# Dealing the maxima pieces anew among a quad's half units, and moving its five value batches

## Chip, cores and metric

The kernel runs on one core of a Trainium2 chip. The metric is the device time of one execution in microseconds (us). In the core TensorE (PE) does matrix products, VectorE (DVE) and ScalarE (ACT) read its results out of PSUM, GpSimd (POOL) moves and gathers, SyncE (SP) issues most DMA transfers, and 16 DMA engines carry them.

## What is computed

A layer norm of x (4 x 1024 x 256) feeds an attention of 16 heads of width 16 and a mixture of 8 experts, two of them chosen for each token; the output is x + attention * silu(experts). Cut to the attention, which the change is about:

```python
S = jnp.einsum('hid,hjd->hij', K, Q) * SCALE          # rows are keys' positions
delta = idx[:, None] - idx[None, :]
S = jnp.where(delta < 0, -jnp.inf, S) + decay         # decay is -delta, causal
C = jax.nn.softmax(S, axis=-1)
attn = jnp.einsum('hij,hjd->hid', C, V)
return attn @ o_w.T + o_b
```

## The kernel before

**Stages.** Layer norm and projections run first (to about 127 us of the profiled span), then the attention in 16 quads of four heads (127 to 601 us), then the experts tile by tile and the output. A quad's work stands in `window(q, ...)`, and a "window" below is the stretch from the first half unit of one quad to the first of the next. q runs from 0 to 15.

**Three kinds of work in a window.** The scores are computed twice. First come the *pieces*: score blocks (L1338, with the diagonal mask added by a small product at L1341) from which DVE takes the row maxima (L988). They are computed one quad ahead. A piece lies in one of three PSUM banks and a new one may be written when DVE has reduced the piece three places earlier (`piece_used`). When piece 37, the last of a quad, is reduced, DVE splits the maxima into three bf16 parts (L993 to L1002); the *maxima* item (L1347) turns them, DVE copies them out (L1008), and SP writes them into the key rows of the next quad (L493), which the next window awaits (`m_in`). Second come 36 *half units* (L1387, mask at L1390): the same scores transposed, less the maxima, which ACT exponentiates (L879); they have three banks of their own. Third come five *batches* (`send_batch`, L1401) of value products, one for each of five types of units; batch k waits for the exponentials of its type. ACT copies a quad's finished output out (L863, `evacuate`) after exponential 5 of the next window.

**Order on TensorE.** It is written out by hand in `window`: half unit i, then one item (two at i = 6, 14 and 30, named in `EXTRA_ITEM`), then the batch whose step is i. `BATCH_STEP` puts batch 0 after half unit 10, batch 1 after 18, batch 2 after 26, batch 3 after 34, and batch 4 after half unit 2 of the next window. The 39 items of window q, numbered j0 to j38 here, are always in the same order: j0 to j23 are pieces 14 to 37 of quad q+1; j24 to j27 pieces 0 to 3 of quad q+2; j28 the maxima of quad q+1; j29 to j38 pieces 4 to 13 of quad q+2. By kind: j1 and j24 hold four masked blocks of 128 columns; j6, j7, j25 and j26 two of 256; j12 to j15, j27 and j29 to j31 one of 384; j20 to j23 and j32 to j35 a masked block of 512; the other 15 pieces an unmasked one. In window 0 one item more, the expert counts, stands at place 20.

**Loads.** The operands of quad q+2 are brought in window q by twelve DMAs of 128 KB (`load_rows`, L484), paced on SP by finished half units; after the sixth stands `store_quad` (L500, L501), eight stores of quad q-1 that wait for `evacuate`. Item j24, the first piece of quad q+2, is the first to read them, and waits for all twelve:

```python
if piece == 0:
    pe.wait_ge(aug_in[(n + d) % AUG], 192 * ((q + d) // AUG) + 192)
```

**Waits of ACT on batches.** Exponential 4 of a window writes where batch 4 of the quad before still reads, so it waits for that batch; the exponentials of types 2, 3 and 4 wait in the same way for batches 0, 1 and 2 of their own quad. POOL's `next_v` waits for batch 4 of the quad before as well.

Of the kernel before, what the change touches and what calls it, by code (L numbers as in the profile page):

```python
# [17 lines left out]
TB = T // P  # L18
# [44 lines left out]
BATCH_STEP = (10, 18, 26, 34, NU + 2)  # L63
EXTRA_ITEM = (6, 14, 30)
# [4 lines left out]
assert len(BATCH_STEP) == NTY  # L69
# [8 lines left out]
INVERT_ITEM = 4  # L78

# [12 lines left out]
assert WIN % PIECE_BANKS == 0 and NU % SCORE_BANKS == 0 and WIN == NU + len(EXTRA_ITEM)  # L92
# [97 lines left out]
def attention_moe_kernel(nc, x, wqT, wkT, wvT, woT, qb, kb, vb, ob, gate, w1, b1, w2, b2, alpha,  # L190
# [5 lines left out]
    with ctx:  # L196
        def sb(name, shape, dt=fp32):
            return ctx.enter_context(nc.sbuf_tensor(name, shape, dt))
# [35 lines left out]
        mask_sb = sb("mask_sb", [P, P], bf16)  # L234
# [9 lines left out]
        zeros = sb("zeros", [P, W])  # L244
# [167 lines left out]
        def many_zeros(n):  # L412
            return bass.AP(zeros[:, :].tensor, zeros[:, :].offset,
                           [list(zeros[:, :].ap[0]), [0, n], [1, D]])
# [7 lines left out]
        def _(sp):  # L422
# [5 lines left out]
            def load_x_chunk(b, c):  # L428
# [8 lines left out]
                     "idb": (idb[:, :], ident_b), "mask": (mask_sb[:, :], mask_neg),  # L437
# [199 lines left out]
        def _(pool):  # L637
            pool.sem_inc(split_done, 8)
            nc.gpsimd.memset(zeros[:, 0:D], 0.0).then_inc(zeros_set, 1)
# [18 lines left out]
            pool.dma_start(xs_t[:, SLOTS - ZERO_TILES:SLOTS, 0:D], many_zeros(ZERO_TILES)).then_inc(xs_zero, 16)  # L658
            pool.dma_start(xs_t[:, SLOTS - ZERO_TILES:SLOTS, D:W], spare[:, :, 0:1].bitcast(fp32),
# [65 lines left out]
            def clear_pads(e, q):  # L725

                pool.wait_ge(pads_ready, 1)
                pool.wait_ge(xs_zero, 32 + 16 * e)
                nc.gpsimd.tensor_copy(zeros[:, D:W].bitcast(i32), spare[:, e, 1:2]).then_inc(zeros_set, 1)
                pool.wait_ge(zeros_set, 4 + e)  # L730
                pool.wait_ge(exp_done, NU * q + PADS_STEP + SCORE_BANKS + 1)
                nc.gpsimd.indirect_dma_start(
                    out=xs_dram, in_=zeros[:, :], in_offset=None,
                    out_offset=bass.IndirectOffsetOnAxis(ap=pad_slot[:, e:e + 1], axis=0)).then_inc(xs_zero, 16)
# [16 lines left out]
            for q in range(MOVE_FROM, FIRST_TAIL):  # L751
                r = q - MOVE_FROM
                first_tile, count = MOVES[r], MOVES[r + 1] - MOVES[r]
                pool.dma_start(x_move[:, 0:count, 0:D], xn_t[:, first_tile:first_tile + count, :]).then_inc(x_moved, 16)
                next_v(q, q % AUG)
                pool.wait_ge(x_moved, 16 * r + 16)
                for k in range(2):
                    pool.wait_ge(scattered, 16 * (2 * first_tile + k * count))
                    nc.gpsimd.tensor_copy(x_move[:, 0:count, D:W].bitcast(i32),
                                          y_row[:, first_tile:first_tile + count, k:k + 1]).then_inc(rows_ready, 1)  # L760
# [11 lines left out]
            pool.dma_start(y_row_of[:, :].bitcast(fp32), xs_t[:, 0:SLOTS, D:W].rearrange("p n o -> p (n o)"),  # L772
# [160 lines left out]
        def _(dve):  # L933
# [49 lines left out]
            def reduce_piece(s, banks, piece):  # L983
                dve.wait_ge(piece_done, s + 1)
                ib, lo, h, heads, width = PIECES[piece]
                src = banks[:, 0:heads * width].rearrange("p (h j) -> p h j", h=heads)
                col_ = ib if lo + width == P * (ib + 1) else TB // 2 + ib
                nc.vector.tensor_reduce(mxa[:, h:h + heads, col_], src, AX.X, ALU.max).then_inc(piece_used, 1)  # L988

            def split_maxima(q, s):  # L990

                dve.wait_ge(piece_used, s + PIECE_BANKS + 1)
                nc.vector.tensor_tensor(mxa[:, :, TB // 2:TB], mxa[:, :, TB // 2:TB], mxa[:, :, TB:],  # L993
                                        ALU.max).then_inc(m_step, 1)
# [51 lines left out]
            ahead_of_windows = iter(list(enumerate(stream(0))))  # L1046

# [12 lines left out]
            dve.wait_ge(consts_in, 16 * NCONST)  # L1060
# [219 lines left out]
        def _(pe):  # L1280
# [50 lines left out]
            def send_piece(n, s, banks, piece):  # L1331
# [3 lines left out]
                for h in range(heads):  # L1335
                    out_ = banks[:, h * width:(h + 1) * width]
                    diagonal = lo + width == P * (ib + 1)
                    ins = nc.tensor.matmul(out_, k_aug[n][0:SCORE_ROWS, h0 + h, ib * P:(ib + 1) * P],  # L1338
                                           q_aug[n][0:SCORE_ROWS, h0 + h, lo:lo + width], start=True, stop=not diagonal)
                    if diagonal:  # L1340
                        ins = nc.tensor.matmul(out_[:, width - P:], idb[:, :], mask_sb[:, :], start=False, stop=True)  # L1341
# [111 lines left out]
            for g, step in enumerate(BATCH_STEP):  # L1453
                if step >= NU:
                    send_batch(NQ - 1, (NQ - 1) % AUG, g)
# [134 lines left out]
```

## Time and profile before

| | us |
|---|---|
| median of 3 runs | 805.32 (805.02 to 805.58) |
| the profiled execution | 801.64 |
| its span, first to last instruction | 799.7 |
| windows 3 to 12, each | 29.71 (window 7: 29.88) |
| windows 0, 1, 2 | 32.82, 30.78, 30.47 |
| windows 13, 14, 15 | 32.40, 27.06, 23.84 |

How to read the profile: the page gives the busy share of each engine over the whole span, and the chain of work that ended last. The windows view gives busy time by stretch, the waits view who waited for whom, the timeline the instructions in order. On PE a matmul is pipelined, so its price is the distance from its start to the next start, not its duration. "PEld" is the load of weights, which runs beside the matmuls. A DMA issued by SP shows as "SPq"; its time to landing is from the issue to the semaphore.

### The profile page before, as it was taken

The page shows a single profiled execution, that of the slowest core. Times are in us where ns is not written, and L with a number is a line of the kernel's source. Part 1 is how long each engine was busy: PE and PEld are TensorE (multiplying, and loading weights), DVE is VectorE, ACT ScalarE, POOL GpSimd, SP SyncE. Part 2 cuts the span into 40 slices and gives each one's busy share as a digit, 9 for nine tenths or more (in the row PEclk, how much of TensorE's full clock was granted, in tenths as well). Part 3 has the DMA queues.
Part 4 walks back from the last instruction along what each step waited for, and adds up shares of the span by engine and source line. Part 5 has one row for each costly group of instructions (what it writes and reads, how often), then busy time and mean ns, then how long its engine had stood idle before and what let it go on. Part 6 is the DMA issues. An engine that isn't in the chain of part 4 may idle for free.

```text
span 799.7 us, 16759 instructions
## 1 busy us (share of the span) xinstructions
PE 746.0 (93%) x5575; PEld 447.8 (56%) x5579; DVE 534.0 (67%) x1084; ACT 520.5 (65%) x1044; POOL 245.4 (31%) x311
## 2 busy tenths in 40 slices
PE   4999998999999999999999999989988999999884
PEld 2555553444554554544544544544437899999763
DVE  2456878788777787787787787787404544444287
ACT  3775556576676676676676676666786566666354
POOL 0442232251123223223223222202134457444300
PEclk9999999999999999999999999999999999999998
DMA  8889935254466476486486476495555765555487
GB/s 206 242 204 270 248 127 126 35 107 96 99 121 122 114 143 131 101 146 134 96 146 141 95 139 138 97 141 115 122 93 163 184 187 170 160 168 164 147 289 248
DMA packets 85253, 119.49 MB, mean 149 GB/s; under 512 B 14175, under 2 KB 58719, under 8 KB 85119
## 3 DMA queue, kind: packets, MB, share of 16 engines
q1 hardware_dynamic: 76654, 94.50, 53.0%
q0 software_dynamic: 8528, 24.07, 9.9%
q8 instruction: 41, 0.67, 0.4%
q14 instruction: 30, 0.25, 0.1%
HBM read 72.61 MB, written 45.52 MB: 148 GB/s over the span
## 4 chain that ended last, share of the span: by engine, by line
PE 66%; DVE 12%; DMA 9%; issue 5%; ACT 3%; SPq 2%; POOL 2%; ACTq 0%; POOLq 0%; DVEq 0%
PE ps L1401 15%; PE ps L1338 13%; PE ps L1387 12%; PE ps L1481 8%; PE ps L1503 7%; DVE mxa L988 7%; DMA arena<-y_dram 3%; PE ps L1390 3%; PE ps L1299 2%; PE ps L1341 2%; PE ps L1464 2%; DMA q_parts<-arena 2%; POOL arena L648 2%; DMA aug<-q_parts 2%; ACT arena L879 1%
## 5 line engine op out<-in xcount | busy, mean ns | idle before, releaser
L988 DVE TENSOR_REDUCE mxa<-ps 128x1 f32<-128x512 f32 (+3 forms) x608 | 363.0, 654 | 93.6 <-PE ps L1341 63.4
L879 ACT ACTIVATE arena<-ps 128x512 f32<-128x512 f32 x576 | 312.1, 604 | 148.5 <-PE ps L1390 130.0
L1338 PE MATMUL ps<-aug 105*128 105x512 bf16 (+3 forms) x768 | 228.8, 327 | 12.8 <-DVE mxa L988 9.5
L1387 PE MATMUL ps<-aug 108*128 108x512 bf16 (+3 forms) x768 | 216.2, 327 | 2.3 <-ACT arena L879 0.8
L1401 PE MATMUL ps<-arena,v_q 128*32 128x512 f32 (+3 forms) x1536 | 140.4, 491 | 3.7 <-ACT arena L879 3.7
L1338 PEld LDWEIGHTS ps<-aug 105*128 105x128 bf16 x768 | 74.8, 98 | 81.9 <-DVE mxa L988 34.6
L1387 PEld LDWEIGHTS ps<-aug 108*128 108x128 bf16 x768 | 66.1, 98 | 84.1 <-issue 32.5
L1390 PE MATMUL ps<-maskT_sb,idb 128*128 128x128 bf16 x512 | 112.4, 220 | 0.0
L1341 PE MATMUL ps<-mask_sb,idb 128*128 128x128 bf16 x512 | 98.6, 219 | 0.0
L764 POOL DMA_INDIRECT xs_dram<-arena,slot x64 | 62.8, 982 | 104.8 <-ACT arena L879 91.0
L785 POOL DMA_INDIRECT y_dram<-arena,y_row_of x71 | 68.8, 969 | 73.2 <-DVE arena L1238 72.1
L1401 PEld LDWEIGHTS ps<-arena,v_q 128*32 128x32 f32 x1536 | 41.1, 109 | 68.4 <-issue 49.6
L1481 PE MATMUL ps<-arena 128*128 128x128 f32 x568 | 75.4, 276 | 2.3 <-ACT arena L894 2.3
L1503 PE MATMUL ps<-w_sb,arena 128*128 x284 | 74.1, 384 | 0.5 <-DVE arena L1238 0.5
L1481 PEld LDWEIGHTS ps<-arena 128*128 128x128 f32 x568 | 69.1, 192 | 3.2 <-ACT arena L894 3.1
L1202 DVE TENSOR_TENSOR arena<-ps,arena 128x256 f32<-128x256 f32 x71 | 30.1, 424 | 48.9 <-PE ps L1481 47.5
L906 ACT ACTIVATE arena<-w_sb 128x512 f32 x71 | 44.7, 629 | 24.6 <-issue 23.8
L1390 PEld LDWEIGHTS ps<-maskT_sb,idb 128*128 128x128 bf16 x512 | 49.9, 97 | 18.1
L648 POOL TENSOR_TENSOR arena<-arena 128x512 bf16<-128x512 f32 x32 | 37.0, 1156 | 67.6 <-ACT arena L817 67.6
L1341 PEld LDWEIGHTS ps<-mask_sb,idb 128*128 128x128 bf16 x512 | 50.2, 98 | 6.4 <-issue 3.3
L1238 DVE TENSOR_TENSOR arena<-ps,arena 128x256 f32<-128x256 f32 x71 | 30.1, 424 | 33.1 <-PE ps L1503 28.6
L1503 PEld LDWEIGHTS ps<-w_sb,arena 128*128 128x128 f32 x284 | 48.6, 190 | 5.4 <-issue 1.3
(136 smaller groups left out, 670.6 us busy)
## 6 DMA issues: line engine op xcount, KB each, us to landing
aug<-k_parts SPq DMA_DIRECT2D x96, 128.0 KB, 4.7
aug<-q_parts SPq DMA_DIRECT2D x96, 128.0 KB, 5.2
arena<-xs_dram SPq DMA_DIRECT2D x71, 128.0 KB, 2.7
arena<-y_dram SPq DMA_DIRECT2D x16, 512.0 KB, 4.9
k_parts<-arena SPq DMA_DIRECT2D x16, 384.0 KB, 5.9
q_parts<-arena SPq DMA_DIRECT2D x16, 384.0 KB, 4.4
arena<-in_x SPq DMA_DIRECT2D x8, 512.0 KB, 6.2
xn_dram<-arena SPq DMA_DIRECT2D x8, 512.0 KB, 8.1
```

Source lines behind the costliest of these rows:

```text
L648: nc.gpsimd.tensor_tensor(parts[c][n][:, 2, :], whole[c][n], parts[c][n][:, 1, :], ALU.subtract).then_inc(split_done, 1)
L764: nc.gpsimd.indirect_dma_start(out=xs_dram, in_=x_move[:, s, :], in_offset=None, out_offset=bass.IndirectOffsetOnAxis(ap=slot[:, first_til ...
L785: nc.gpsimd.indirect_dma_start(out=y_dram, in_=ysb[n % STEP], in_offset=None, out_offset=bass.IndirectOffsetOnAxis(ap=y_row_of[:, n:n + 1] ...
L879: nc.scalar.activation(probs[SLOT[k, u]][:, half], score_bank(q, i), ACT.Exp).then_inc(exp_done, 1)
L988: nc.vector.tensor_reduce(mxa[:, h:h + heads, col_], src, AX.X, ALU.max).then_inc(piece_used, 1)
L1338: ins = nc.tensor.matmul(out_, k_aug[n][0:SCORE_ROWS, h0 + h, ib * P:(ib + 1) * P], q_aug[n][0:SCORE_ROWS, h0 + h, lo:lo + width], start=T ...
L1341: ins = nc.tensor.matmul(out_[:, width - P:], idb[:, :], mask_sb[:, :], start=False, stop=True)
L1387: ins = nc.tensor.matmul(out_, q_aug[n][0:ALL_ROWS, h, jb * P:(jb + 1) * P], k_aug[n][0:ALL_ROWS, h, i0:i0 + hi - lo], start=True, stop=lo ...
L1390: ins = nc.tensor.matmul(out_[:, 0:P], idb[:, :], maskT_sb[:, :], start=False, stop=True)
L1401: ins = nc.tensor.matmul(ps[2 * HD * h:2 * HD * (h + 1), 6 * BANK + lo:6 * BANK + hi], v_q[n][:, jb, h, :], probs[SLOT[k, u]][:, at_:at_ + ...
L1481: ins = nc.tensor.matmul(bank(2 + j % 2)[:, m * P:(m + 1) * P], w1_now[j % 2][:, k, m * P:(m + 1) * P], xgT[j % CH][:, k * P:(k + 1) * P], ...
L1503: ins = nc.tensor.matmul(bank(6 + j % 2)[:, 0:D], hid[j % CH][:, k * P:(k + 1) * P], w2_sb[:, e * KT + k, :], start=(k == 0), stop=(k == K ...
```

## The change

Only TensorE's order is changed in substance. The table `ITEMS_AFTER` says how many items follow each half unit (0 to 3), `BATCH_AFTER` after which half unit a batch is sent, and `ITEMS_BEFORE_BATCH` how many of that step's items go ahead of it. Batch 4 of the quad before moves from half unit 2 to 4, batch 0 stays at 10, batch 1 moves from 18 to 22, batch 2 stays at 26, batch 3 moves from 34 to 33. The order of the items among themselves and that of the half units are the same, and so are the programs of DVE and ACT. Written out (h half unit, j item, B batch), the window becomes:

```
h0 h1 j0 j1 h2 h3 j2 j3 h4 j4 [B4 of the quad before] j5 h5 j6 j7 h6 h7 j8 j9 h8 j10 h9 j11 h10 [B0]
j12 j13 h11 j14 h12 j15 h13 h14 j16 j17 h15 j18 h16 h17 j19 h18 j20 h19 j21 h20 h21 j22 h22 j23 j24 [B1]
j25 h23 j26 h24 j27 j28 h25 h26 j29 [B2] h27 h28 j30 h29 j31 j32 h30 j33 h31 h32 j34 j35 h33 j36 [B3]
h34 j37 h35 j38
```

Beside it, small things: the mask and a block of zeros share one tile (`blank`), so the mask begins at another address; a row of `xs_dram` holds its index in column 0 and its data in columns 1 to 256, where the index was last; DVE's wait for the constants stands ahead of its second batch of projections, where it stood behind the last; `masked_by_vector` always returns False, so the path it opens on DVE is not taken; `MERGED` is 4, so the merge of maxima has the columns it had.

```diff
-BATCH_STEP = (10, 18, 26, 34, NU + 2)
-EXTRA_ITEM = (6, 14, 30)
+ITEMS_AFTER = (0, 2, 0, 2, 2, 2, 0, 2, 1, 1, 2, 1, 1, 0, 2, 1, 0, 1, 1, 1, 0, 1, 3, 1, 2, 0, 1, 0, 1, 2, 1, 0, 2, 1, 1, 1)
+BATCH_AFTER = (4, 10, 22, 26, 33)
+ITEMS_BEFORE_BATCH = (1, 0, 2, 1, 1)
...
+def masked_by_vector(piece):
+
+    ib, lo, h, heads, width = PIECES[piece]
+    return False
...
-        mask_sb = sb("mask_sb", [P, P], bf16)
...
-        zeros = sb("zeros", [P, W])
+        blank = sb("blank", [P, W + P // 2])
+        zeros = blank[:, 1:W]
+        wide_mask = blank[:, :].bitcast(bf16)
+        mask_sb = wide_mask[:, 2 * W:2 * W + P]
...
-                sp.dma_start(xg[j], xs_dram[bass.ts(n, P), 0:D]).then_inc(xg_in[j], 16)
+                sp.dma_start(xg[j], xs_dram[bass.ts(n, P), 1:W]).then_inc(xg_in[j], 16)
...
+            dve.wait_ge(zeros_set, 1)
+            dve.wait_ge(consts_in, 16 * NCONST)
...
             def window(q, n, base, items, first=False):
                 sent = 0
-                pe.wait_ge(m_in, 48 * q + 48)
-                for i in range(NU):
-                    half_unit(q, n, i)
-                    for _ in range(2 if i in EXTRA_ITEM or first and i == COUNTS_STEP else 1):
+
+                def send_items(count):
+                    nonlocal sent
+                    for _ in range(count):
                         held = q == NQ - 2 and i < MAXIMA_STEP and sent < len(items) and items[sent][0] == "maxima"
                         if sent < len(items) and not held:
                             send(q, n, base + sent, piece_bank(base, sent), items[sent])
                             sent += 1
-                    if i in BATCH_STEP:
-                        send_batch(q, n, BATCH_STEP.index(i))
-                    elif NU + i in BATCH_STEP and not first:
-                        send_batch(q - 1, (n - 1) % AUG, BATCH_STEP.index(NU + i))
-
+
+                pe.wait_ge(m_in, 48 * q + 48)
+                for i in range(NU):
+                    half_unit(q, n, i)
+                    count = ITEMS_AFTER[i] + (first and i == COUNTS_STEP)
+                    if i not in BATCH_AFTER:
+                        send_items(count)
+                        continue
+                    b = BATCH_AFTER.index(i)
+                    send_items(ITEMS_BEFORE_BATCH[b])
+                    if b > 0:
+                        send_batch(q, n, b - 1)
+                    elif not first:
+                        send_batch(q - 1, (n - 1) % AUG, NTY - 1)
+                    send_items(count - ITEMS_BEFORE_BATCH[b])
```

## Rows read from the trace of the kernel before

**Rows 1.** The page's busy time and share of each engine.
```profile
PE 746.0 (93%) x5575; PEld 447.8 (56%) x5579; DVE 534.0 (67%) x1084; ACT 520.5 (65%) x1044; POOL 245.4 (31%) x311
```

**Rows 2.** Windows view, windows 6 and 13: busy us (count) by engine, granted clock, DMA share.
```profile
309.88:339.59 29.71, 29.39 (x259) 14.67 (x258) 23.52 (x44) 20.36 (x38) 8.84 (x12) 1.00 0.66 126
518.03:550.43 32.40, 29.65 (x258) 14.64 (x256) 26.16 (x48) 21.17 (x38) 2.84 (x2) 1.00 0.99 160
```

**Rows 3.** PE's timeline in window 6: start, duration, line, shape.
```profile
312.87 0.38 PE L1338 MATMUL ps<-aug 105*128 105x512 bf16 x1
313.09 0.38 PE L1387 MATMUL ps<-aug 108*128 108x512 bf16 x1
313.30 0.22 PE L1390 MATMUL ps<-maskT_sb,idb 128*128 128x128 bf16 x1
313.36 0.38 PE L1338 MATMUL ps<-aug 105*128 105x512 bf16 x1
...
317.34 1.92 PE L1401 MATMUL ps<-arena,v_q 128*32 128x512 f32 x16
319.20 0.39 PE L1387 MATMUL ps<-aug 108*128 108x384 bf16 x2
```

**Rows 4.** The same timeline about j24, the piece before the maxima item, and the next window.
```profile
327.53 0.23 PE L1338 MATMUL ps<-aug 105*128 105x128 bf16 x1
...
329.98 0.34 PE L1338 MATMUL ps<-aug 105*128 105x384 bf16 x1 [0.30 <-DVE mxa L988]
...
339.59 0.38 PE L1387 MATMUL ps<-aug 108*128 108x512 bf16 x1
```

**Rows 5.** DVE's timeline in window 6: reductions and the split of the maxima.
```profile
313.29 5.47 DVE L988 TENSOR_REDUCE mxa<-ps 128x1 f32<-128x512 f32 x9 [0.73 <-PE ps L1338]
...
328.14 0.17 DVE L993 TENSOR_TENSOR mxa<-mxa 128x16 f32<-128x16 f32 x1
...
329.23 2.35 DVE L988 TENSOR_REDUCE mxa<-ps 128x4 f32<-128x512 f32 x4
```

**Rows 6.** ACT's timeline in window 6: the evacuation.
```profile
314.59 1.03 ACT L863 ACTIVATE arena<-ps 128x1024 f32<-128x1024 f32 x1
```

**Rows 7.** SP's issues in window 6: load 7, load 12.
```profile
318.59 0.33 SPq L484 DMA_DIRECT2D aug<-k_parts  x1
...
321.90 0.32 SPq L484 DMA_DIRECT2D aug<-q_parts  x1
```

**Rows 8.** Tile view of the twelve loads, windows 3 and then 6: us to landing.
```profile
DMA to landing us min/median/max: 3.2/3.8/5.0
...
DMA to landing us min/median/max: 4.1/4.9/5.6
```

**Rows 9.** The chain that ended last: start, us, what; the last load of windows 7 and 12.
```profile
351.61 6.16 DMA aug<-q_parts
...
500.34 6.19 DMA aug<-q_parts
```

**Rows 10.** Waits for these loads in windows 0, 7 and 13: us in total, times, longest.
```profile
PEld ps L1338 <- DMA aug<-q_parts: 0.4, 1, 0.4
...
PEld ps L1338 <- DMA aug<-q_parts: 0.9, 1, 0.9
...
PEld ps L1338 <- DMA aug<-q_parts: 1.6, 1, 1.6
```

**Rows 11.** PE's timeline: j24 in window 13.
```profile
538.60 0.23 PE L1338 MATMUL ps<-aug 105*128 105x128 bf16 x1 [1.27 <-DMA aug<-q_parts]
```

**Rows 12.** Windows view, window 6 from 2 to 15 us after its start.
```profile
311.88:324.88 13.00, 13.00 (x103) 5.81 (x99) 11.12 (x20) 9.48 (x18) 4.50 (x7) 1.00 1.02 165
```

**Rows 13.** ACT's timeline in window 15, which has no items: its idle time before each stretch.
```profile
584.82 4.03 ACT L879 ACTIVATE arena<-ps 128x512 f32<-128x512 f32 x8 [1.02 <-PE ps L1390]
```

**Rows 14.** PE's longest idle time late in the kernel, and the granted clock behind it.
```profile
761.25 0.59 PE L1516 MATMUL ps<-arena,before_sb 128*128 128x512 bf16 x1 [3.91 <-DVE arena L1261]
...
761.10:764.51 3.41, 3.27 (x8) 2.67 (x9) 3.41 (x8) 2.96 (x7) 0.00 (x0) 0.50 0.71 226
```

More of the change, by code:

```diff
@@ L68 @@
 PIECE_BANKS = SCORE_BANKS = 3
-assert len(BATCH_STEP) == NTY
+assert len(BATCH_AFTER) == len(ITEMS_BEFORE_BATCH) == NTY and len(ITEMS_AFTER) == NU
 SHARES_STEP = 27
@@ L78 @@
 INVERT_ITEM = 4
+def masked_by_vector(piece):
+    ib, lo, h, heads, width = PIECES[piece]
+    return False
+MERGED = len({ib for piece, (ib, lo, *_) in enumerate(PIECES) if 0 < lo and not masked_by_vector(piece)})
 def stream(ahead, more=2):
@@ L91 @@
 WIN = len(stream(1))
-assert WIN % PIECE_BANKS == 0 and NU % SCORE_BANKS == 0 and WIN == NU + len(EXTRA_ITEM)
+assert WIN % PIECE_BANKS == 0 and NU % SCORE_BANKS == 0 and WIN == sum(ITEMS_AFTER)
 AUG = 3
@@ L412, in many_zeros @@
         def many_zeros(n):
[L413 to L414 removed]
+            return bass.AP(zeros.tensor, zeros.offset, [list(zeros.ap[0]), [0, n], [1, D]])
         best, first, second, gap, gexp, where, norm, low = col
@@ L436, in _ @@
                      "wv": (wvg_sb[:, :, 0:D], weights(wvT)), "gate": (wvg_sb[:, :, D:D + E], weights(gate)),
-                     "idb": (idb[:, :], ident_b), "mask": (mask_sb[:, :], mask_neg),
+                     "idb": (idb[:, :], ident_b), "mask": (mask_sb, mask_neg),
                      "maskT": (maskT_sb[:, :], mask_negT), "before": (before_sb[:, :], before),
@@ L638, in _ @@
             pool.sem_inc(split_done, 8)
-            nc.gpsimd.memset(zeros[:, 0:D], 0.0).then_inc(zeros_set, 1)
+            nc.gpsimd.memset(zeros, 0.0).then_inc(zeros_set, 1)
             for n in range(AUG):
@@ L728, in clear_pads @@
                 pool.wait_ge(xs_zero, 32 + 16 * e)
-                nc.gpsimd.tensor_copy(zeros[:, D:W].bitcast(i32), spare[:, e, 1:2]).then_inc(zeros_set, 1)
+                nc.gpsimd.tensor_copy(blank[:, 0:1].bitcast(i32), spare[:, e, 1:2]).then_inc(zeros_set, 1)
                 pool.wait_ge(zeros_set, 4 + e)
@@ L732, in clear_pads @@
                 nc.gpsimd.indirect_dma_start(
-                    out=xs_dram, in_=zeros[:, :], in_offset=None,
+                    out=xs_dram, in_=blank[:, 0:W], in_offset=None,
                     out_offset=bass.IndirectOffsetOnAxis(ap=pad_slot[:, e:e + 1], axis=0)).then_inc(xs_zero, 16)
@@ L753, in _ @@
                 first_tile, count = MOVES[r], MOVES[r + 1] - MOVES[r]
-                pool.dma_start(x_move[:, 0:count, 0:D], xn_t[:, first_tile:first_tile + count, :]).then_inc(x_moved, 16)
+                pool.dma_start(x_move[:, 0:count, 1:W], xn_t[:, first_tile:first_tile + count, :]).then_inc(x_moved, 16)
                 next_v(q, q % AUG)
@@ L758, in _ @@
                     pool.wait_ge(scattered, 16 * (2 * first_tile + k * count))
-                    nc.gpsimd.tensor_copy(x_move[:, 0:count, D:W].bitcast(i32),
+                    nc.gpsimd.tensor_copy(x_move[:, 0:count, 0:1].bitcast(i32),
                                           y_row[:, first_tile:first_tile + count, k:k + 1]).then_inc(rows_ready, 1)
@@ L987, in reduce_piece @@
                 col_ = ib if lo + width == P * (ib + 1) else TB // 2 + ib
-                nc.vector.tensor_reduce(mxa[:, h:h + heads, col_], src, AX.X, ALU.max).then_inc(piece_used, 1)
+                if masked_by_vector(piece):
+                    row = banks[:, 0:width]
+                    begin = NEG
+                    if lo > 0:
+                        dve.wait_ge(piece_used, s - HQ + PIECE_BANKS + 1)
+                        begin = mxa[:, h, TB // 2 + ib:TB // 2 + ib + 1]
+                    nc.vector.tensor_tensor_reduce(
+                        out=row, in0=row, in1=wide_mask[:, 2 * W + P - width:2 * W + P], scale=1.0, scalar=begin,
+                        op0=ALU.add, op1=ALU.max, accum_out=mxa[:, h, ib:ib + 1]).then_inc(piece_used, 1)
+                else:
+                    nc.vector.tensor_reduce(mxa[:, h:h + heads, col_], src, AX.X, ALU.max).then_inc(piece_used, 1)
             def split_maxima(q, s):
                 dve.wait_ge(piece_used, s + PIECE_BANKS + 1)
-                nc.vector.tensor_tensor(mxa[:, :, TB // 2:TB], mxa[:, :, TB // 2:TB], mxa[:, :, TB:],
-                                        ALU.max).then_inc(m_step, 1)
+                split, merged = slice(TB // 2, TB // 2 + MERGED), slice(TB, TB + MERGED)
+                nc.vector.tensor_tensor(mxa[:, :, split], mxa[:, :, split], mxa[:, :, merged], ALU.max).then_inc(m_step, 1)
                 dve.wait_ge(m_step, 4 * q + 1)
@@ L1336, in send_piece @@
                     out_ = banks[:, h * width:(h + 1) * width]
-                    diagonal = lo + width == P * (ib + 1)
+                    diagonal = lo + width == P * (ib + 1) and not masked_by_vector(piece)
                     ins = nc.tensor.matmul(out_, k_aug[n][0:SCORE_ROWS, h0 + h, ib * P:(ib + 1) * P],
@@ L1340, in send_piece @@
                     if diagonal:
-                        ins = nc.tensor.matmul(out_[:, width - P:], idb[:, :], mask_sb[:, :], start=False, stop=True)
+                        ins = nc.tensor.matmul(out_[:, width - P:], idb[:, :], mask_sb, start=False, stop=True)
                 ins.then_inc(piece_done, 1)
@@ L1452, in _ @@
                 window(q, q % AUG, first_item(q), items_of(q), first=q == 0)
-            for g, step in enumerate(BATCH_STEP):
-                if step >= NU:
-                    send_batch(NQ - 1, (NQ - 1) % AUG, g)
+            send_batch(NQ - 1, (NQ - 1) % AUG, NTY - 1)
             pe.wait_ge(piece_used, LAST_ITEM + PIECE_BANKS)
```

7 lines of the change are left out of this document (3 added, 4 removed).

## The prediction

> **What bounds the kernel now.** I read the page first: PE is busy 93% of the span, DVE 67%, ACT 65% [rows 1], so PE sets the pace, if the 93% means work. The windows view tells where to look: each window from 3 to 12 takes 29.71 us, with DVE busy 23.52 and ACT 20.36 of it [rows 2]. These ten are alike, and their start is the zero of all "+" times below. Next I took PE's timeline in window 6 apart, by the distance from one start to the next. An unmasked piece of 512 columns takes 0.22, a half unit 0.21 plus 0.06 for its mask, a batch of 16 or 24 matmuls 1.86 and about 0.1 ahead of it [rows 3]; the short batch 4 takes 1.1 in the same way. Reckoned by columns, the pieces come to: 15 unmasked at 0.22, eight masked of 512 at 0.28, eight of 384 at 0.22, four of two 256s at 0.34, two of four 128s at 0.46, and the maxima 0.16.
>
> Before j24 in the changed order stand 23 half units (four unmasked: 6.1), j0 to j23 (6.0), B4 and B0 (1.1 and 1.95): 15.15 us. From j24 to the next window stand 13 half units (3.6), j24 to j38 (3.95) and B1 to B3 (5.85): 13.4. A window without waits would be 28.55 us. It takes 29.71, so **1.15 us of PE's waits per window** is all that a new order can win there. The largest stands between j26 and j27, 0.30 idle behind DVE [rows 4]: just before, DVE spent 1.09 us on the split of the maxima (328.14 to 329.23), with each reduction taking 0.60 [rows 5]. The others are a few tenths about +5 to +8, where ACT's evacuation (1.03) and DVE's backlog meet [rows 6].
>
> The last view is that of the loads, because j24 waits for all twelve of them. In window 6 load 12 is issued at +12.02 (321.90) [rows 7] and lands up to 5.6 us later [rows 8], at +17.6; j24 starts at 327.53, +17.65 [rows 4]. **The loads already arrive just in time**, or late: in windows 7 and 12 they land at 357.77 and 506.53, both +18.2 [rows 9], and in window 7 j24's weights wait 0.9 for them [rows 10]. In window 3 load 12, issued at +12.03, lands 5.0 later, at +17.05 [rows 8].
>
> **The change, part by part.** *Batch 1 from half unit 18 to 22.* PE's 1.95 us of B1 then cover DVE's 1.09 of split, and the wait at j27 goes. Following DVE at 0.60 a piece with three banks, I find a bank free at every piece of the long stretch from B0 to B1, and even its last piece would wait at most 0.3, inside the wait that comes next. Gain 0.65 a window.
>
> *Items dealt unevenly, batch 4 to half unit 4.* It halves the backlog about +5 to +8. Exponential 4 must now wait for B4. B4 would end at +3.8, exponential 5 ends by +4.9, and the evacuation ends at +5.85 against 315.62, +5.74, now [rows 6]; half unit 9 then waits about 0.12 for ACT. Gain 0.35, with a tenth left as waits. Batch 3 one step earlier has its exponentials 0.4 us ahead of need: nothing. POOL's `next_v`, held by B4 one microsecond longer, delays scatters that nothing in a window waits for: nothing.
>
> *Where j24 now comes.* By these parts alone a window would fall to 28.7 us. But B1, which stood ahead of j24, now stands behind it, and the waits ahead of it are gone: j24 is due at 15.15 + 0.12 = **+15.3, not +17.65**. The loads do not come earlier. They are paced by half units, which reach the fifteenth at +11.5 in both orders; loads 7 to 12 (from 318.59 on) [rows 7] stand behind the eight stores, and these behind the evacuation, which moves by +0.1. Nor is the pace of issue the limit: from +2 to +15 the 16 DMA engines are taken up entirely (share 1.02) [rows 12]. So PE stands at j24 for some 2.3 us, with B1 and half unit 23 queued behind it and ACT and DVE running dry. The window becomes landing + 0.05 + 13.4. Landings that rows show are +17.05, +17.6 and twice +18.2; in the windows without such a wait I take 17.4, between the earliest seen and j24's present time without a wait, 17.53. The mean over windows 3 to 12 is 17.55, the new window 31.0, against a mean of 29.73 now: **+1.28 us ten times, +12.8**. Bounds: all landings at 17.05 give +0.77 each, all at 18.2 +1.92.
>
> The Trainium skill speaks against this figure. "DMA: Bandwidth & Descriptors", section "Anatomy of one DMA — SWDGE (gpsimd) path", gives a DMA about 2.0 us plus its bytes at 436 GB/s; an estimate from it for 128 KB is 2.3 us, by which load 12 would land at +14.3, ahead of the new j24, and the first rival below would be the outcome. The rows show 5.0 to 6.2 us for this load among its neighbours, and they decide.
>
> *The other windows.* Window 0: the counts stand before B1, so here j24 comes behind B1; it waits for the loads already now [rows 10], would do so again, and with the waits behind it gone the window gains 1.0. Windows 1 and 2 are long (30.78, 30.47) from DVE's extra expert steps; they end at 17.1 + 0.05 + 13.4 = 30.55: -0.2 and +0.1. Window 13: DMA share 0.99 [rows 2], j24 waits 1.6 [rows 10] and starts at 538.60, +20.6 [rows 11]; plus 13.4 is 34.0 against 32.40: +1.5. Window 14 has no j24: -0.2. Window 15 has no items: ACT idles about 1.0 before each stretch behind a batch [rows 13], and one of these four goes when B1 follows six half units that ACT can still work on, while B3 ahead of two half units gives half back: -0.5.
>
> *The small edits.* The moved index column and the mask's new address change no count of instructions or bytes; the transposes of `x_move`, whose rows already begin at odd multiples of 4 bytes, stand for both, and I take 0, with -0.5 to +0.5 as bounds. DVE's earlier wait stands where PE waits for the same constants: 0.
>
> **Sum.** 12.8 - 1.0 - 0.2 + 0.1 + 1.5 - 0.2 - 0.5 = +12.5 on the profiled 801.64, hence 814.1. The median of the runs lies 3.7 above that execution, which I carry over: 805.32 + 12.5 = **817.8 us**. With the bounds of the landing (0.77 to 1.92 a window) and half a microsecond for the rest, 812 to 825.
>
> **Rivals.** *The loads come in time.* If the order of the half units drew the landings to +15.3 or earlier, windows 3 to 12 would fall to 28.7 (-10.3), windows 0 to 2 by 1.0 each, 13 to 15 by 1.2 together: -14.5, **791 us**, faster. It decides from a landing 1.75 us earlier than the earliest seen. For it: half unit 3 ends 1.3 us earlier, so load 4 is issued earlier. Against: with the engines full from +2 on, an earlier issue only waits in the queue. *The loads come partly in time*: traffic at the head of the window falls into the longer window before, and landings move to about +16.3; then 16.3 + 13.45 = 29.75, no change, about **805**. *The clock falls in the new wait*: after PE stood idle 3.91 us the granted clock was 0.50 for 3.41 us [rows 14], which would cost 1.7 us in each of some 11 windows, **836**. Against: waits to 1.6 us left it at 1.00 (window 13) [rows 2, 10]; 2.3 lies nearer to those. *The change does not do what it says*, that is, batches stay where they were in effect, is excluded by the order written out: PE works in program order.
>
> **How the numbers follow.** Forecast 0.76, loads in time 0.13, partly 0.05, clock 0.06. The range takes in the forecast's bounds and the partly-in-time case, 804 to 825, leaving out 0.19. About 0.2% can be told from no change here. Faster takes the first rival and a third of the second, 0.15; same the middle of the second, 0.03; slower the rest, 0.82.
>
> **What the changed profile would show.** If I am right: windows 3 to 12 at 30.5 to 31.7 us, in each a wait of PE for the `q_parts` loads of 1.7 to 2.9 us just ahead of the second four-block piece, no idle between j26 and j27, and j24 at +17 to +18.2. If windows are near 28.7 and the waits for the loads are gone, the step "the loads do not come earlier" is wrong. If the wait is there and windows still gain, the tally of 13.4 us is.

## Result and the profile after

| | before | after |
|---|---|---|
| median of 4 runs, us | 805.17 (802.2 to 805.58) | 822.07 (821.11 to 827.46) |
| ratio, 95% interval | | 1.0232 (1.0181 to 1.0283) |
| profiled execution, its span | 801.64, 799.7 | 821.11, 819.1 |
| granted clock over the span | 0.995 | 0.986 |
| start of window 0 | 126.66 | 127.22 |
| windows 0, 1, 2 | 32.82, 30.78, 30.47 | 34.05, 30.81, 31.72 |
| windows 3 to 12, mean | 29.73 | 31.06 (30.59 to 33.14) |
| windows 13, 14, 15 | 32.40, 27.06, 23.84 | 36.61, 26.25, 23.19 |

The kernel became slower by 16.9 us on the medians, and by 19.5 between the two profiled executions. The highest of the four runs, 827.46, has also the lowest granted clock, 0.979 against 0.985 and 0.986. The windows account for the second figure: +0.56 before window 0, +1.23, +0.03 and +1.25 in windows 0 to 2, +13.34 in windows 3 to 12, +4.21 in window 13, -1.46 in 14 and 15, 19.2 in all.

The page of the changed kernel, its busy times and then the two lines of the chain that ended last (shares of the span by engine, by line):

```profile
PE 747.2 (91%) x5578; PEld 451.0 (55%) x5579; DVE 536.2 (65%) x1084; ACT 512.1 (63%) x1044; POOL 245.0 (30%) x311
...
PE 66%; DMA 14%; DVE 8%; issue 5%; ACT 3%; POOL 2%; SPq 1%; ACTq 0%; POOLq 0%; DVEq 0%
PE ps L1423 16%; PE ps L1360 13%; PE ps L1409 12%; DMA aug<-q_parts 9%; PE ps L1511 8%; PE ps L1533 7%; DVE mxa L1009 4%; PE ps L1363 3%; PE ps L1412 3%; DMA arena<-y_dram 3%; PE ps L1321 2%; PE ps L1494 2%; DMA q_parts<-arena 2%; POOL arena L659 2%; ACT arena L890 1%
```

PE's busy time has hardly moved against [rows 1], but its share fell, and the loads into `aug`, of which the chain of the kernel before held two [rows 9], are now 9% of it. The chain, taken over windows 5 to 10, has one such load in each (start, us, what):

```profile
299.77 5.64 DMA aug<-q_parts
330.86 5.59 DMA aug<-q_parts
361.90 5.28 DMA aug<-q_parts
392.62 5.23 DMA aug<-q_parts
423.30 4.76 DMA aug<-q_parts
453.89 5.66 DMA aug<-q_parts
```

PE's timeline in window 6, which starts at 318.82 (start, duration, line, shape, and in brackets the idle time ahead and what ended it):

```profile
333.89 0.38 PE L1360 MATMUL ps<-aug 105*128 105x512 bf16 x1
334.11 0.22 PE L1363 MATMUL ps<-blank,idb 128*128 128x128 bf16 x1
336.50 0.23 PE L1360 MATMUL ps<-aug 105*128 105x128 bf16 x1 [2.17 <-DMA aug<-q_parts]
...
337.07 1.93 PE L1423 MATMUL ps<-arena,v_q 128*32 128x384 f32 x24
...
339.90 0.38 PE L1409 MATMUL ps<-aug 108*128 108x512 bf16 x1
340.18 0.33 PE L1360 MATMUL ps<-aug 105*128 105x384 bf16 x1
```

The third line is j24: +17.68, as in [rows 4] (+17.65), but PE has stood 2.17 us in front of it, and batch 1 (337.07) follows where it used to precede. Load 12 was issued at 330.86, +12.04, against +12.02 in [rows 7], and landed 5.59 later, against 5.6 in [rows 8]. So load 12 did not move at all in this window. The idle time between j26 and j27 of [rows 4] is gone (340.18, no bracket): DVE's split ran in the shade of batch 1, as intended. What was saved elsewhere went into the wait.

The windows view of the changed kernel: windows 0, 4, 6 and 13 (stretch, length, busy us and count of PE, PEld, DVE, ACT, POOL, granted clock, DMA share, GB/s):

```profile
127.22:161.28 34.06, 29.69 (x252) 14.47 (x252) 28.71 (x58) 20.73 (x40) 6.90 (x15) 1.00 0.46 71
254.59:287.73 33.14, 30.49 (x258) 15.36 (x257) 23.61 (x45) 19.74 (x39) 8.78 (x12) 0.95 0.58 112
318.82:349.86 31.04, 28.87 (x258) 14.79 (x257) 23.54 (x45) 19.74 (x39) 8.79 (x12) 1.00 0.59 120
534.45:571.06 36.61, 32.14 (x259) 15.53 (x257) 25.81 (x48) 20.30 (x39) 2.72 (x2) 0.91 0.85 144
```

Against [rows 2], window 6 is 1.33 us longer with 0.5 us less of PE's work in it. Windows 4 and 13 show a thing that no window of the kernel before had, a granted clock below 1.00; they are taken up below.

### The profile page after: what moved, and what is told of

Its sections match the earlier page's. It is cut to its first block, busy times and chain, and to the rows that moved or that the text cites. A ratio compares the mean times of both kernels' runs of the same rounds, so it can differ in the third digit from the quotient of the medians.

```text
span 819.1 us, 16762 instructions
## 1 busy us (share of the span) xinstructions
PE 747.2 (91%) x5578; PEld 451.0 (55%) x5579; DVE 536.2 (65%) x1084; ACT 512.1 (63%) x1044; POOL 245.0 (30%) x311
## 4 chain that ended last, share of the span: by engine, by line
PE 66%; DMA 14%; DVE 8%; issue 5%; ACT 3%; POOL 2%; SPq 1%; ACTq 0%; POOLq 0%; DVEq 0%
PE ps L1423 16%; PE ps L1360 13%; PE ps L1409 12%; DMA aug<-q_parts 9%; PE ps L1511 8%; PE ps L1533 7%; DVE mxa L1009 4%; PE ps L1363 3%; PE ps L1412 3%; DMA arena<-y_dram 3%; PE ps L1321 2%; PE ps L1494 2%; DMA q_parts<-arena 2%; POOL arena L659 2%; ACT arena L890 1%
## 5 line engine op out<-in xcount | busy, mean ns | idle before, releaser
L890 ACT ACTIVATE arena<-ps 128x512 f32<-128x512 f32 x576 | 303.4, 608 | 175.8 <-PE ps L1412 157.6
L1360 PE MATMUL ps<-aug 105*128 105x512 bf16 (+3 forms) x768 | 219.2, 328 | 33.1 <-DMA aug<-q_parts 26.8
L1409 PE MATMUL ps<-aug 108*128 108x512 bf16 (+3 forms) x768 | 203.4, 327 | 2.2 <-ACT arena L890 1.0
L1423 PE MATMUL ps<-arena,v_q 128*32 128x512 f32 (+3 forms) x1536 | 143.2, 499 | 2.9 <-ACT arena L890 2.9
L1363 PE MATMUL ps<-blank,idb 128*128 128x128 bf16 x512 | 99.4, 221 | 0.0
L1363 PEld LDWEIGHTS ps<-blank,idb 128*128 128x128 bf16 x512 | 50.5, 99 | 7.9 <-issue 3.3
```

Source lines behind the costliest of these rows:

```text
L890: nc.scalar.activation(probs[SLOT[k, u]][:, half], score_bank(q, i), ACT.Exp).then_inc(exp_done, 1)
L1409: ins = nc.tensor.matmul(out_, q_aug[n][0:ALL_ROWS, h, jb * P:(jb + 1) * P], k_aug[n][0:ALL_ROWS, h, i0:i0 + hi - lo], start=True, stop=lo ...
L1423: ins = nc.tensor.matmul(ps[2 * HD * h:2 * HD * (h + 1), 6 * BANK + lo:6 * BANK + hi], v_q[n][:, jb, h, :], probs[SLOT[k, u]][:, at_:at_ + ...
```

## Experiments

Two theories stand against each other. By the first, j24's place against the landing of load 12 decides everything: batch 1 behind j24 leaves 1.95 us less work ahead of it, and PE stands. By the second, the loss lies in the new deal of items, in batches 4 and 3, or in the small edits. All times are medians of 2 to 10 runs, ratios against the kernel before on the same chip.

**One number changed.** Batch 1 stays after half unit 22, but one of that step's items stands ahead of it instead of two; j24 comes behind the batch.

```diff
-ITEMS_BEFORE_BATCH = (1, 0, 2, 1, 1)
+ITEMS_BEFORE_BATCH = (1, 0, 1, 1, 1)
```

> The changed kernel, with batch 1 sent ahead of j24 instead of behind it (one item ahead of the batch at half unit 22 instead of two). If the loss is PE's wait for the twelve loads at j24: the batch's 1.95 us fill that wait, j24 is due at +17.2, the wait shrinks to 0 to 0.5 us, windows 3 to 12 take 28.8 to 29.4 us, and the total is 794 to 801 us, below the kernel before. If the uneven deal or the later batch 4 costs by itself: windows stay near 31 and the total near 820. If the moved index column or the mask's address costs: the total stays above 815. If the clock falls because of the wait: no stretch of half clock in the windows any more.

Measured: 800.09 us, 0.9946 (0.9927 to 0.9966). Its windows 6 and 7, and PE's wait for the loads in each (us in total, times, longest):

```profile
310.00:339.31 29.31, 28.94 (x258) 14.78 (x257) 23.52 (x45) 19.85 (x39) 8.79 (x12) 1.00 0.60 127
339.31:369.38 30.07, 28.94 (x258) 14.78 (x257) 23.39 (x45) 19.84 (x39) 8.79 (x12) 1.00 0.66 126
```

```profile
PE ps L1360 <- DMA aug<-q_parts: 0.3, 1, 0.3
...
PE ps L1360 <- DMA aug<-q_parts: 1.0, 1, 1.0
```

One item's place is worth 22 us. The total is in the expected range, the windows are not all: 3 to 12 took 28.95 to 30.12, where 28.8 to 29.4 was expected. With the batch in front, j24 comes at about the time at which the loads land, and only their scatter is left as waits of 0 to 1.1 us.

**The mirror image, from the old deal.** Two kernels have the changed kernel's code with the old deal of items and batches 4 and 3 in their old places; batch 1 alone is moved, ahead of j24 in the one (first diff) and behind it in the other (second).

```diff
-ITEMS_AFTER = (0, 2, 0, 2, 2, 2, 0, 2, 1, 1, 2, 1, 1, 0, 2, 1, 0, 1, 1, 1, 0, 1, 3, 1, 2, 0, 1, 0, 1, 2, 1, 0, 2, 1, 1, 1)
-BATCH_AFTER = (4, 10, 22, 26, 33)
-ITEMS_BEFORE_BATCH = (1, 0, 2, 1, 1)
+ITEMS_AFTER = (1, 1, 1, 1, 1, 1, 2, 1, 1, 1, 1, 1, 1, 1, 2, 1, 1, 1, 1, 1, 1, 1, 1, 1, 1, 1, 1, 1, 1, 1, 2, 1, 1, 1, 1, 1)
+BATCH_AFTER = (2, 10, 22, 26, 34)
+ITEMS_BEFORE_BATCH = (1, 1, 0, 1, 1)
```

```diff
-ITEMS_BEFORE_BATCH = (1, 1, 0, 1, 1)
+ITEMS_BEFORE_BATCH = (1, 1, 1, 1, 1)
```

> The old deal and the old places of batches 0, 2, 3 and 4, with batch 1 alone moved from half unit 18 to 22, ahead of j24. If the split of the maxima is hidden under batch 1 as I worked out: no idle between j26 and j27, windows 29.0 to 29.3 (up to 29.9 where the loads land late), total 797 to 802. If the gain of the new order comes from the uneven deal and not from batch 1: windows stay at 29.6 to 29.7 and the total at 804.

> The same, with batch 1 one place later: behind j24. If the place of batch 1 against j24 is the whole loss: j24 is due some 1.9 us earlier than its loads, PE waits 1.7 to 2.3 us there, windows 3 to 12 take 30.8 to 31.2 us, total 814 to 822. If the loss needs the uneven deal or the later batch 4: windows stay under 29.8 and the total under 806.

Measured: ahead 794.71, 0.988 (0.9851 to 0.9908); behind 815.95, 1.015 (1.0122 to 1.0177). So 21 us again, without the new deal. Behind, windows 3 to 12 took 30.28 to 31.22, with waits of 1.16 to 1.83 at j24 from window 4 on, somewhat less than expected; the total is in its range. Ahead, they took 29.05 to 29.48, most of them 29.05 or 29.06, 0.65 less than before, which is the price that the prediction gave the split. The total is below the 797 to 802 expected, since windows 1, 2 and 13 to 15 became shorter too (window 13 took 31.60 instead of 32.40). PE's timeline of this kernel, and then DVE's, over the split:

```profile
322.94 1.93 PE L1423 MATMUL ps<-arena,v_q 128*32 128x384 f32 x24
324.84 0.23 PE L1360 MATMUL ps<-aug 105*128 105x128 bf16 x1
...
326.83 0.33 PE L1360 MATMUL ps<-aug 105*128 105x384 bf16 x1
```

```profile
324.05 0.17 DVE L1015 TENSOR_TENSOR mxa<-mxa 128x16 f32<-128x16 f32 x1
...
324.92 0.19 DVE L1023 TENSOR_TENSOR msplit<-mrest,msplit 128x32 bf16<-128x32 f32 x1
```

DVE's split (324.05 to 325.11) now falls inside batch 1 but for 0.3 us, and j27 at 326.83 has no idle time ahead of it.

**The small edits alone.** The changed kernel's code with all three tables set to the old order, the counts of items as in the two kernels above.

```diff
-BATCH_AFTER = (4, 10, 22, 26, 33)
-ITEMS_BEFORE_BATCH = (1, 0, 2, 1, 1)
+BATCH_AFTER = (2, 10, 18, 26, 34)
+ITEMS_BEFORE_BATCH = (1, 1, 1, 1, 1)
```

> The changed kernel with the tables set so that TensorE's order is that of the kernel before; the index column, the mask's tile and the earlier wait of VectorE stay. If the order is all that counts: 805 us, within 1.5 of the kernel before, windows at 29.71. If the small edits cost: over 808, up to all of the loss, 822.

Measured: 804.64, 1.0017 (0.9996 to 1.0038), windows of 29.71. The small edits cost nothing that can be measured, and the loss is all in the order.

**What sets the landing.** Is it SP, which issues eight stores ahead of loads 7 to 12, or the DMA engines, which carry both? In the changed kernel and in the one before, the stores were moved behind the twelve loads.

```diff
                 for g in range(2 * len(K_PART)):
-                    if g == STORE_AT and q > 0:
-                        store_quad(q - 1)
...
                         load_rows(q + 2, (n + 2) % AUG, g)
+                if q > 0:
+                    store_quad(q - 1)
```

> The changed kernel, with the eight stores of the quad before issued behind the twelve loads instead of between the sixth and the seventh. If the loss is the wait for the loads: loads 7 to 12 no longer stand behind 272 KB of stores, the last lands at +14.5 to +16 instead of +17.2 to +17.8, PE's wait at j24 falls to at most 0.8 us, windows 3 to 12 take 28.7 to 29.5, total 793 to 803 us. If the DMA engines are the limit whatever the order, the landing moves by under 0.5 us and the total stays at 815 or more. If the deal itself costs, 815 or more as well, with the wait gone.

> The kernel before, with the eight stores behind the twelve loads. The kernel before waits for the loads only in windows 0, 7, 12 and 13 to speak of. If my reading is right: windows stay at 29.7 and the total is 802 to 805 us, so the loads are no limit in the old order. If the loads hold up the old order too (j24 is held by them in windows where no wait shows): windows of 29.2 or less and a total under 799.

Measured: 809.82, 1.0069 (1.0041 to 1.0097), for the changed kernel; 804.96, 0.9999 (0.9976 to 1.0022), for the kernel before. The second is as expected: there the landing costs little, because j24 is reached as late as that. The first missed the 793 to 803 expected of it. j24 moved from +17.54 to +16.48 in the mean of windows 3 to 12, 1.06 us, where at least 1.2 was expected of the landing; and window 13 still took 36.96, with a stretch of half clock in it. The chain of that kernel in window 7, which starts at 342.76:

```profile
354.80 3.78 DMA aug<-q_parts
358.57 0.62 issue
359.19 0.23 PE ps L1360
```

Load 12 is still issued at +12.04. Its landing, as the chain has it, comes 3.78 later, where it took 5.28 in this window of the changed kernel; j24 starts another 0.62 after it, for which the chain names no cause. But the edit moves more than bytes: SP now issues loads 7 and 8 at +6.21 and +6.87, where it was +8.73 and +9.11; loads 9 to 12 go out as before (load 7 in window 7 of the changed kernel, then here):

```profile
358.59 0.33 SPq L495 DMA_DIRECT2D aug<-k_parts  x1
...
348.97 0.32 SPq L495 DMA_DIRECT2D aug<-k_parts  x1
```

So the stores hold up the landing of load 12 at an unchanged issue, but whether by their bytes or by the later issue of loads 7 and 8, this run does not part. Without them j24 still starts 1.1 us after it is due (+15.38, by the run with half the loads below). Whether loads issued earlier would be there in time was not tried: SP paces them by half units.

The other direction: four more stores of 64 KB ahead of the eight, in windows 2 to 12 (their bytes go to a tensor that nobody reads).

```diff
+                if 1 <= q <= 11:
+                    for h in range(HQ):
+                        rows = slice(32 * h, 32 * h + 32)
+                        sp.dma_start(more_dram[q, rows, :], wo_sb[rows, :, :].rearrange("p k n -> p (k n)")
+                                     ).then_inc(more_stored, 16)
```

> The changed kernel with four more stores of 64 KB each (a constant tile, into memory that nothing reads) ahead of the stores of windows 2 to 12: the suspected cost doubled. If the bytes ahead of loads 7 to 12 set the landing: it moves by about 1.0 us (what the late stores gave back), PE's wait at j24 grows from 2.0 to 3.0 us. If the issues on SP set it: by 1.3 or more, as four issues take 0.33 each. If neither matters, the windows stay at 31. And on the clock: a wait of 2.9 us ahead of j24 was followed by half clock in window 4, waits of 2.5 and less were not; if that border is right, most of these windows show a stretch of 0.5, they take 33 to 34 us, and the total is 840 to 855; if the clock stays at 1.00, 32 us and about 833.

Measured: 855.09, 1.0629 (1.0594 to 1.0663), at the upper end of the 840 to 855 expected with half clock. j24 moved to +19.19 in the mean, 1.65 us later, nearer to what the account by issues gave than to the 1.0 by bytes; both have a part in it, as in window 7 load 12 went out at +12.8, 0.8 later, and took 6.08 instead of 5.28. The run shows something else as well: window 7 below took 33.92, more than j24's start and 13.4, and the second line, a stretch of it, has the granted clock at 0.51 over 3.41 us. Ahead of it stands the wait of the second fence, from PE's timeline.

```profile
364.67:398.59 33.92, 30.48 (x258) 15.34 (x257) 23.61 (x45) 19.73 (x39) 8.84 (x12) 0.95 0.60 119
...
385.00:388.41 3.41, 3.41 (x29) 1.50 (x18) 0.54 (x2) 0.00 (x0) 0.00 (x0) 0.51 0.00 0
```

```profile
383.62 0.23 PE L1369 MATMUL ps<-aug 105*128 105x128 bf16 x1 [3.44 <-DMA aug<-q_parts]
```

j24 comes at +18.95 here; plus 13.36 is 32.31, and the window took 1.61 more. All eleven windows with the extra stores show the same: waits of 3.04 to 4.45 at j24, and 3.41 us at half clock behind each.

**The loads taken away.** Six of the twelve loads are left out from quad 3 on, so that the scores there come in part from rows of an earlier quad.

```diff
-                    if q + 2 < NQ:
+                    if q + 2 < NQ and (q + 2 < AUG or g < len(K_PART)):
...
-                        pe.wait_ge(aug_in[(n + d) % AUG], 192 * ((q + d) // AUG) + 192)
+                        pe.wait_ge(aug_in[(n + d) % AUG], 96 * ((q + d) // AUG) + 192)
```

> The changed kernel, order untouched, with six of the twelve loads left out from quad 3 on (so the scores are made from old rows; j24 waits for the six that are left). This takes away what PE waits for and nothing of PE's work. If that wait is the whole loss: windows 1 to 12 take 28.7 to 29.0 us, window 13 under 31, and the total is 790 to 797 us without a stretch of half clock in the windows. If something else in the new order costs as well, windows stay over 29.5.

Measured: 790.85, 0.9831 (0.9806 to 0.9856). Window 6 and window 13, and PE's timeline at j24 in window 6:

```profile
307.75:336.47 28.72, 28.72 (x258) 14.79 (x257) 23.53 (x45) 19.74 (x39) 8.85 (x12) 1.00 0.40 103
510.28:540.24 29.96, 29.51 (x259) 14.61 (x258) 25.73 (x48) 20.29 (x39) 2.88 (x2) 1.00 0.91 150
```

```profile
323.13 0.22 PE L1360 MATMUL ps<-aug 105*128 105x128 bf16 x1
```

This is the changed order as it would be if the loads came in time: j24 at +15.38, most of windows 3 to 12 at 28.72 (windows 1 and 2 at 29.85 and 30.49, more than expected), no half clock in any. It is the first rival's case, priced at 791. The new order would gain by itself; the loads do not allow it.

**Both, and the best.** Batch 1 ahead of j24 and the stores late, with the new deal and with the old; and last, the old deal with the stores late in windows 1 to 11 alone, because window 13, where the engines are taken up already (DMA share 0.99 in [rows 2]), became longer when they moved in the kernel before (34.02 for 32.40).

The first two put together edits shown above; the diff is the last one's, to the kernel with batch 1 alone ahead of j24.

```diff
-                    if g == STORE_AT and q > 0:
+                    if g == STORE_AT and q >= NQ - 4:
                         store_quad(q - 1)
...
+                if 0 < q < NQ - 4:
+                    store_quad(q - 1)
```

> The changed kernel with both edits: batch 1 ahead of j24, and the eight stores behind the twelve loads. With j24 due at +17.25 and the loads landed by +16.1 to +17.1 (as with late stores alone), no wait for the loads should be left in windows 3 to 12: 28.8 to 28.9 us each, which is the tally of 28.55 with its tenth or two of waits. Total 791 to 796 us. If something else than the loads holds windows over 29 us in the new order (a wait for ACT or for DVE), they stay at 29.2 or more and the total at 798 or more.

> The old deal with batch 1 alone at half unit 22, ahead of j24, and the eight stores behind the twelve loads. Batch 1 alone left waits for the loads in windows 4, 6, 11 and 13 (0.2, 0.05, 0.25, 0.95 us). If the later stores take them away as they did in the uneven deal: windows 3 to 12 at 29.05, total 793 to 795 us, at best 1 us under batch 1 alone. If the stores in their new place hold up window 13 (as they did in the kernel before with late stores: 34.0 against 32.4): 795 to 797, no gain or a small loss.

> Batch 1 alone at half unit 22, ahead of j24, and the stores behind the loads in windows 1 to 11 only; from window 12 on they stand where they stood. Windows 3 to 12 should take 29.05 to 29.5 and window 13 again 31.6 instead of 33.6. If window 13's loss with late stores came from the stores' place, the total is 1 to 2 us under that kernel, 793 to 794.5 us, and not above batch 1 alone; if it came from something else in window 13, 795 to 796.

Measured: 797.71, 0.9915 (0.9892 to 0.9937); 795.5, 0.9897 (0.9877 to 0.9916); 793.78, 0.9886 (0.9862 to 0.9909). Windows 7 and 0 of the first, and then window 6 of the second:

```profile
338.60:367.56 28.96, 28.87 (x259) 14.77 (x258) 23.43 (x45) 19.85 (x39) 8.81 (x12) 1.00 0.59 130
127.53:161.87 34.34, 29.53 (x252) 14.52 (x253) 27.96 (x58) 20.73 (x40) 6.97 (x15) 1.00 0.45 70
```

```profile
307.12:336.17 29.05, 29.05 (x258) 14.64 (x257) 23.42 (x44) 20.34 (x38) 8.84 (x12) 1.00 0.65 128
```

With batch 1 ahead of j24, the new deal wins 0.10 in a steady window (28.95 for 29.05) and loses 1.5 in window 0: 34.34 here, against 32.83 with the old deal. So the first missed its 791 to 796: steady windows took 28.95 where 28.8 to 28.9 was expected, and window 0 was left out of the reckoning. Window 13 took 33.57 in the second and 32.59 in the third, where 31.6 was expected of it; one profile of each does not part the stores' place from the scatter of the landing. The late stores add nothing that can be told apart once batch 1 stands in front: 795.5 and 793.78 beside 794.71. **The best version moves batch 1 alone, ahead of j24**, at 0.988 of the time before (0.985 to 0.991).

## Why the prediction was right, and where it was off

**The sign and its mechanism held.** 817.8 was forecast with 812 to 825 for that case; 822.07 came. *PE stands at j24, batch 1 queued behind it*: 1.73 to 2.65 us in windows 3 to 12, where 1.7 to 2.9 was said. *j24 due at +15.3*: +15.38 without the late loads. *13.4 us from j24 to the next window*: 13.36 in each of windows 1 to 12 without half clock. *The loads do not come earlier*: j24 at +17.54 in the mean of windows 3 to 12, forecast +17.6. The ten windows lost 13.3 us, 1.6 of it by the half clock in window 4; the other 11.7 stand against 12.8 forecast.

That the total came within 4.3 us is in part luck. On the profiled executions +19.5 came where +12.5 was summed; the terms below are what was missing. The medians differ by only 16.9, because the profiled execution lies 3.5 below the median in the kernel before and 1.0 below it in the changed one.

The load's price carried the sign. By the Trainium skill, "DMA: Bandwidth & Descriptors", section "Anatomy of one DMA — SWDGE (gpsimd) path", whose fit is for GpSimd's transfers, one such load was estimated at 2.3 us. The chain shows 4.8 to 6.1 in windows 3 to 12 of the changed kernel, 3.75 to 4.53 without the stores in front (j24 starting up to 0.62 after that), and 5.98 to 6.5 with four stores more, so the measurement decides. The eight stores in front are a part of it; how the rest divides between the other loads and the load itself, no run shows.

**The clock was weighed as all or nothing.** The rival had it fall in every window for 836, or in none. It fell in two. Windows view of the changed kernel over these stretches, and PE's timeline at the wait ahead of each:

```profile
274.00:277.41 3.41, 3.41 (x27) 1.50 (x20) 0.47 (x2) 0.00 (x0) 0.00 (x0) 0.50 0.00 0
553.90:560.70 6.80, 5.62 (x39) 2.60 (x40) 0.92 (x2) 0.00 (x0) 0.00 (x0) 0.50 0.94 259
```

```profile
272.75 0.23 PE L1360 MATMUL ps<-aug 105*128 105x128 bf16 x1 [2.65 <-DMA aug<-q_parts]
...
555.08 0.29 PE L1360 MATMUL ps<-aug 105*128 105x128 bf16 x1 [4.06 <-DMA aug<-q_parts]
```

In window 4 the wait was 2.65 us, and 33.14 is 1.6 more than 18.16 + 13.36. The prediction said that 2.3 lies nearer to the harmless 1.6 than to 3.91; that was right for nine windows of the ten, but the landings scatter by 0.9 and one went over. The price of 1.7 a fall, from [rows 14], was right for window 4; what failed was to set one wait for all windows where the bounds of the landing already gave waits from 1.75 to 2.9.

**Window 13** was forecast at 34.0 and took 36.61. j24 came at +20.62, as [rows 11] have it (+20.6), and 20.62 + 13.36 is 33.98. The other 2.6 us are the 6.8 us at half clock behind a wait of 4.06. That a long wait was coming could be reckoned: +20.6 less +15.3 is 5.3, above the 3.91 of [rows 14]. (It was 4.06, as j24 falls due later in this window: +16.61 in the kernel with half the loads.) The step that failed is this one, a term of +1.5 that came to +4.2. Where that wait is gone, in the kernel with half the loads, window 13 took 29.96.

**Window 0** was forecast at -1.0 and came out at +1.2. The forecast had j24 wait for the loads again; it does not, it follows batch 1 without idle time (148.63, no bracket). In the old order items stand singly between half units, j2 ahead of half unit 3; in the new one j2 and j3 stand behind it. In this first window ACT's exponentials start late (their table is loaded from 127.80 to 129.08). PE's timeline at its start and at j24, and then DVE's in the window; the last line is DVE's in the kernel before, its longest idle time at the start of this window:

```profile
129.84 0.39 PE L1409 MATMUL ps<-aug 108*128 108x512 bf16 x1 [1.01 <-ACT arena L890]
...
146.77 1.93 PE L1423 MATMUL ps<-arena,v_q 128*32 128x384 f32 x24
148.63 0.23 PE L1360 MATMUL ps<-aug 105*128 105x128 bf16 x1
```

```profile
130.49 0.69 DVE L1009 TENSOR_REDUCE mxa<-ps 128x1 f32<-128x512 f32 x1 [1.06 <-PE ps L1360]
...
155.59 4.05 DVE L1009 TENSOR_REDUCE mxa<-ps 128x1 f32<-128x384 f32 x7 [2.04 <-PE ps L1363]
...
129.93 0.69 DVE L988 TENSOR_REDUCE mxa<-ps 128x1 f32<-128x512 f32 x1 [0.27 <-PE ps L1338]
```

Half unit 3 waits 1.01 for ACT, j2 and j3 with it, and DVE, busy 28.7 of the window's 34, has nothing to reduce for 1.06. The runs part the two causes. The counts put the items of this window one place back, so the kernels with batch 1 "behind j24" have it here between the quad's last piece and j24, and those with batch 1 "ahead of j24" have it ahead of that last piece too. With the old deal, window 0 took 32.83 with batch 1 ahead of the last piece and 32.24 behind it, so the gain from the batch is there, 0.6 of the 1.0 forecast; the kernels that pay elsewhere miss it here. With the new deal it took 34.31 and 34.34 in the first place, and 34.05, 33.71 and 33.71 in the second: the deal costs 1.5 to 1.8 there, and this term was missing. That DVE's idle times are the way by which it costs them is read from the trace, and no run tested it.

**The uneven deal** was priced at 0.35 a window. In the run with half the loads, windows took 28.72, which is 0.33 below the 29.05 of batch 1 alone. With batch 1 ahead of j24 only 0.10 shows, because there PE loses 0.24 more just before the maxima (PE's timeline in the kernel with both edits, and then DVE's):

```profile
357.78 0.22 PE L1363 MATMUL ps<-blank,idb 128*128 128x128 bf16 x1
358.08 0.23 PE L1369 MATMUL ps<-idb,msplit 128*96 128x128 bf16 x1
```

```profile
355.95 0.19 DVE L1023 TENSOR_TENSOR msplit<-mrest,msplit 128x32 bf16<-128x32 f32 x1
356.64 1.29 DVE L1009 TENSOR_REDUCE mxa<-ps 128x4 f32<-128x512 f32 x2 [0.50 <-PE ps L1363]
```

The split is done at 356.14, so it is not what holds the maxima. They need the bank of the piece three places earlier, j25, and DVE, which gets to j24 at 356.64, is done with j25 only 1.29 later, at 357.93. In the new deal the maxima follow j27 directly, without the half unit that stood between them.

So the term fits the order of the change, as far as a run with fewer loads can tell, and less than a third of it is left in the order that pays.

**Smaller terms.** The small edits were put at 0, and the run with them alone shows no difference. Window 2 was put at +0.1 and came out at +1.25: its j24 starts at +18.36, where +17.1 was taken for the landing. Load 12 is issued at +13.65 there (205.74), with the stores moved behind it at +13.64 (206.10), and with the old deal and batch 1 behind j24 at +12.70 (202.79), in a window of 30.47. So it is the new deal again and not the stores: the half units that pace the loads come later in this window. What slows them was not tried. That the half units "reach the fifteenth at +11.5 in both orders" holds for the steady windows alone. Windows 14 and 15, -0.7 forecast, gave -1.46. The start of window 0 moved by 0.56; over all profiled executions it lies between 126.50 and 127.98, and this last is the old order too (the kernel before with its stores late), so that is scatter.

## What to carry to other kernels

When work is moved to fill one engine's gaps, look for the wait just behind it that is fixed in time by something else, here twelve loads: the work moved past it was its cover, and the gaps closed ahead of it only lengthen it. Reckon when the waiting instruction falls due in the new order, and compare that with the landing in each window and not with its mean, because a few tenths more in one window can bring the half clock in. When an order gains and loses at once, move the parts apart: one batch placed on the other side of one piece turned +2.3% into -0.5%, and without the new deal of items into -1.2%.

## What the runs showed of the hardware beyond expectation

- **A stall in the middle of the windows can bring the half clock, and its length alone does not settle it.** Behind waits of PE at j24 of up to 2.23 us (changed kernel, windows 3 and 5 to 12) the granted clock stayed at 1.00, 2.4 GHz. Behind each of the longer ones in all kernels, from 2.65 to 4.54, it fell to 0.5, 1.2 GHz, for 3.41 us in windows 2 to 12 and for 6.8 us in window 13; the cost was 1.6 to 1.7 us and 2.5 to 2.9 us. But late in the kernel with the old deal, batch 1 ahead of j24 and the stores late, PE stood for 3.55 us at the place of [rows 14] and the clock stayed at 1.00 (first two lines). And in window 0 of the kernel with four more stores it fell at +7.9 with no stall over 1.01 us in the window before it (third line), while the same start of that window left it at 1.00 in the changed kernel.

```profile
753.41 0.38 PE L1546 MATMUL ps<-arena,before_sb 128*128 128x512 bf16 x1 [3.55 <-DVE arena L1283]
...
753.41:757.00 3.59, 3.56 (x16) 2.85 (x17) 3.59 (x8) 3.24 (x7) 0.00 (x0) 1.00 0.64 209
...
135.78:139.19 3.41, 3.41 (x14) 1.10 (x16) 3.41 (x9) 1.72 (x3) 0.00 (x0) 0.50 1.08 127
```

- **A load's time to landing depends on the transfers issued in front of it.** The same 128 KB, issued at the same +12.04 of window 7 with and without eight stores ahead (loads 7 and 8 going out later with them), took 5.28 and 3.78 us by the chain, and j24 started at +17.36 and +16.43. In window 13, over which the DMA share is 0.85, it took 7.96.
- **A mean hides the scatter.** With the issues alike to 0.1 us, j24 came between +17.23 and +18.16 in windows 3 to 12.
